# Bias row as the router's 65th row, chosen sets marked by replacement, and a new set-up order in a gated attention and FP4 MLP kernel

## What is computed

```python
q = layernorm(x) @ W_q.T + b_q
scores = (q @ desc_router.T) / sqrt(256)          # 64 sets
scores = where(set named by one of the token's 4 entries, scores, -inf)
keep the two largest; weights = softmax over them
x = x + tanh(g_xattn) * weights @ ctx
h = layernorm(x)
x = x + tanh(g_ffn) * ((gelu_tanh(h @ Wg.T) * (h @ Wu.T)) @ Wd.T)
```

## Time and profile before

| | us |
|---|---|
| median of 3 runs | 310.67 |
| profiled execution | 311.26 |
| its span | 309.5 |

### The profile page before, as it was taken

One profiled execution on the slowest core, in us unless ns is written; L12 is line 12 of the kernel. 1 busy time (PEld: TensorE's weight loads), 2 busy tenths in 40 slices (PEclk: granted clock), 3 DMA queues, 4 the chain that ended last, 5 costly groups with the idle time before them and its releaser, 6 DMA issues.

```text
span 309.5 us, 4648 instructions
## 1 busy us (share of the span) xinstructions
PE 302.0 (98%) x1537; PEld 251.0 (81%) x1537; DVE 223.6 (72%) x478; ACT 155.9 (50%) x287; POOL 144.8 (47%) x138
## 2 busy tenths in 40 slices
PE   6998999999999999999999999999999999999996
PEld 4777888787788788888888888888888888888885
DVE  3999999899985669687676678777676565544545
ACT  3476665657455453435555453444654533444341
POOL 3447455636742342876353325866442233432421
PEclk9999999999999999999999999999999999999999
DMA  6970440020000021326240111424130001110102
GB/s 184 253 186 0 150 124 0 0 37 1 0 2 0 2 34 17 77 57 123 70 101 3 17 17 26 94 53 85 63 94 0 0 15 26 26 40 0 37 0 68
DMA packets 47288, 16.11 MB, mean 52 GB/s; under 512 B 38944, under 2 KB 44448, under 8 KB 47264
## 3 DMA queue, kind: packets, MB, share of 16 engines
q1 hardware_dynamic: 44576, 12.92, 18.0%
q0 software_dynamic: 864, 2.10, 2.5%
q10 hardware_dynamic: 1824, 0.79, 1.1%
HBM read 11.08 MB, written 3.15 MB: 46 GB/s over the span
## 4 chain that ended last, share of the span: by engine, by line
PE 78%; issue 7%; POOL 6%; DVE 4%; ACT 2%; DMA 2%; SPq 0%; DVEq 0%; POOLq 0%
PE ring_ps L1317 49%; PE acc_ps L1351 17%; PE acc_ps L1364 4%; PE att_ps L1364 3%; POOL act_lo L525 3%; POOL w_nat L507 2%; DMA x_sb<-in_x_dram 2%; PE att_ps L1219 1%; POOL w_nat L518 1%; PE ring_ps L1302 1%; ACT act L695 1%; DVE act L1006 0%; DVE act L1000 0%; DVE x_sb L1157 0%; ACT act L691 0%
## 5 line engine op out<-in xcount | busy, mean ns | idle before, releaser
L525 POOL TENSOR_TENSOR act_lo<-act,act_hi 128x512 fp32r<-128x512 f32 x63 | 82.1, 1302 | 118.8 <-ACT act_hi L702 118.6
L1317 PE MATMUL ring_ps<-xt_hi,w_hi 128*128 128x512 f32 (+1 forms) x264 | 103.8, 394 | 1.0 <-ACT xt_hi L675 0.7
L1317 PE MATMUL ring_ps<-xt_hi,w_lo 128*128 128x512 f32 (+1 forms) x264 | 100.9, 384 | 0.0
L1317 PE MATMUL ring_ps<-xt_lo,w_hi 128*128 128x512 f32 (+1 forms) x264 | 100.2, 384 | 0.0
L691 ACT ACTIVATE act<-ring_ps 128x512 f32<-128x512 f32 x64 | 38.1, 596 | 84.2 <-PE ring_ps L1317 83.8
L1000 DVE SCALAR_TENSOR_TENSOR act<-act,ring_ps 128x512 f32<-128x512 f32 x64 | 43.7, 683 | 39.1 <-ACT act L691 38.9
L1006 DVE SCALAR_TENSOR_TENSOR act<-act,ring_ps 128x512 f32<-128x512 f32 x64 | 43.8, 685 | 27.2 <-ACT act L695 25.9
L1317 PEld LDWEIGHTS ring_ps<-xt_hi,w_hi 128*128 128x128 f32 x264 | 49.7, 188 | 11.1 <-issue 1.2
L1317 PEld LDWEIGHTS ring_ps<-xt_lo,w_hi 128*128 128x128 f32 x264 | 49.0, 188 | 10.3 <-DVE xt_lo L938 0.2
L695 ACT ACTIVATE act<-act 128x512 f32<-128x512 f32 x64 | 40.5, 632 | 32.7 <-DVE act L1000 32.7
L1317 PEld LDWEIGHTS ring_ps<-xt_hi,w_lo 128*128 128x128 f32 x264 | 49.8, 188 | 8.3
(11 more groups left out here) (129 smaller groups left out, 331.9 us busy)
## 6 DMA issues: line engine op xcount, KB each, us to landing
x_t<-in_x_dram SPq DMA_DIRECT2D x48, 32.0 KB, 2.1
w_nat<-w_nat SPq DMA_DIRECT2D x96, 16.0 KB
out_dram<-x_sb SPq DMA_DIRECT2D x6, 256.0 KB, 2.2
x_sb<-in_x_dram SPq DMA_DIRECT2D x1, 1024.0 KB, 8.4
ln_dram<-normed SPq DMA_DIRECT2D x16, 64.0 KB, 2.2
w_nat<-ln_dram SPq DMA_DIRECT2D x16, 64.0 KB, 2.0
packed<-L_ffn_gate_W_packed_dram SPq DMA_DIRECT2D x3, 256.0 KB, 2.9
packed<-n_L_ffn_up_W_packed_dram SPq DMA_DIRECT2D x3, 256.0 KB, 3.3
```

The lines of the kernel that those rows point to most:

```text
L525: pool.tensor_tensor(act_lo[:, s % RING, :], act[:, s % ACT_RING, :], act_hi[:, s % RING, :].bitcast(F32), ALU.subtract).then_inc(inter_lo, 1)
L1317: i = pe.matmul(into[:, tok], wt[:, n, w], xt[:, c % 2, k, tok], start=(k, j) == order[0], stop=(k, j) == order[-1])
```

## The change

The b_q row is loaded as row 64 of the router tile, by the second load of ACT's queue, and the tokens by the third instead of POOL's first. The router's transposes now wait for b_q too and give 65 columns; `spread_bias` multiplies the 65th column by the others, and DVE's two instructions on b_q are gone. SCORE_SCALE is halved and later factors doubled.

For sequences 0 to 3, ACT computes tanh(2 s - s0 - s1) of all 64 scores, a half of the tokens at a time, and adds 1 (`soft`); DVE writes CHOSEN over the two largest with two `match_replace` (`marked`; entries 2 to 7 of the eight are set to a spare value that also stands behind the scores), and one instruction takes `soft` where `marked` is CHOSEN. For sequences 4 to 7 the way through indices stays.

The set-up orders of PE, ACT, DVE and POOL are new, with other numbers of zero products. Score(2) moves from unit 2 of the loop into the set-up, ahead of the last first product. Declarations of semaphores and plain slices `0:SETS` are left out below.

```diff
-MASKED = -3.0e38
+MASKED = -1.0e38
+CHOSEN = 2.0e38
+SPARE = 3.0e38
...
-    SCORE_SCALE = float(D) ** -0.5
+    SCORE_SCALE = 0.5 * float(D) ** -0.5
...
-        router_sb = sb("router_sb", [SETS, D])
+        router_sb = sb("router_sb", [SETS + 1, D])
...
-        set_bias = sb("set_bias", [SETS, 1])
-        router_t = sb("router_t", [P, KT, SETS])
+        router_t = sb("router_t", [P, KT, SETS + 1])
...
-        scores = sb("scores", [P, CB, HALVES, SETS])
+        scores = sb("scores", [P, CB, HALVES, SETS + 6])
...
-        picked = choice[:, 0:CB * HALVES * 2 * SETS].rearrange("p (q h k n) -> p q h k n", q=CB, h=HALVES, k=2)
+        soft = choice[:, 0:CB * HALVES * SETS].rearrange("p (q h n) -> p q h n", q=CB, h=HALVES)
+        marked = choice[:, CB * HALVES * SETS:CB * HALVES * SETS + HALVES * (SETS + 6)].rearrange("p (h n) -> p h n", h=HALVES)
...
+        BIAS_AT = KT * (SETS + 1)
...
-            sp.dma_start(router_sb[:, :], router).then_inc(router_loaded, 16)
+            sp.dma_start(router_sb[0:SETS, :], router).then_inc(router_loaded, 16)
...
-            pool.dma_start(tok_sb[:, :, :], token_sets.rearrange("(p h) k -> p h k", h=HALVES)).then_inc(tokens_loaded, 16)
...
+            pool.memset(scores[:, :, :, SETS:], SPARE).then_inc(spares_made, 1)
...
-            for i in range(2):
-                scale_rows_of(1, i)
+            scale_rows_of(1, 0)
+            scale_rows_of(1, 1)
+            root_1(CB)
...
-            root_1(CB)
-            for i in range(2):
-                scale_rows_of(2, i)
+            scale_rows_of(2, 0)
+            scale_rows_of(2, 1)
...
-            sc.dma_start(bq_sb[:, :], b_q.rearrange("(a d) -> a d", a=1).to_broadcast([SETS, D])).then_inc(small_loaded, 16)
+            sc.dma_start(router_sb[SETS:SETS + 1, :], b_q.rearrange("(a d) -> a d", a=1)).then_inc(small_loaded, 16)
+            sc.dma_start(tok_sb[:, :, :], token_sets.rearrange("(p h) k -> p h k", h=HALVES)).then_inc(tokens_loaded, 16)
...
+                q = b % CB
...
-                for k, factor in enumerate((-0.5, 0.5)):
-                    i = sc.activation(lead_tanh[:, b % CB, :, k], lead[:, b % CB, :], ACT.Tanh, scale=factor)
-                i.then_inc(lead_tanh_ready, 1)
+                if b >= BY_ROWS:
+                    for k, factor in enumerate((-1.0, 1.0)):
+                        i = sc.activation(lead_tanh[:, q, :, k], lead[:, q, :], ACT.Tanh, scale=factor)
+                    i.then_inc(lead_tanh_ready, 1)
+                    return
+                for h in range(HALVES):
+                    i = sc.activation(soft[:, q, h, :], scores[:, q, h, 0:SETS], ACT.Tanh, bias=lead[:, q, h:h + 1], scale=2.0)
+                i.then_inc(soft_made, 1)
+                sc.wait_ge(soft_made, b + 1)
+                sc.activation(soft[:, q, :, :], soft[:, q, :, :], ACT.Identity, bias=1.0).then_inc(lead_tanh_ready, 1)
...
                 sc.wait_ge(wq_summed, e + 1)
                 sc.activation(wq_sb[:, e, :], wq_sb[:, e, :], ACT.Identity, bias=wq_sum[:, e:e + 1],
                               scale=-float(D)).then_inc(wq_centered, 1)
-            x_t_out(0)
             sc.wait_ge(score_w_done, 1)
             sc.activation(score_w[:, :, :], acc_ps[:, 1, 0:KT * SETS].rearrange("p (k n) -> p k n", k=KT),
                           ACT.Copy, scale=-SCORE_SCALE / D).then_inc(score_w_copied, 1)
+            x_t_out(0)
             x_t_out(1)
-            lead_out(0)
             compact(0)
             sc.wait_ge(gates_loaded, 16 * 2)
             sc.activation(gates[:, :], gates_in[:, :], ACT.Tanh).then_inc(gates_ready, 1)
+            lead_out(0)
             sc.wait_ge(gates_ready, 1)
             sc.activation(half_gate[:, :], gates[:, :], ACT.Copy, scale=0.5).then_inc(gates_ready, 1)
             probs_out(0)
-            lead_out(1)
             sc.wait_ge(down_scales_loaded, 16)
             sc.activation(scales_sb[:, :, 4:6, :].rearrange("p r a b -> p a r b"), down_scales_sb[:, :, :, :],
                           ACT.Copy).then_inc(down_scales_placed, 1)
+            lead_out(1)
             compact(1)
             rows_high(0)
+            rows_high(1)
             normalise(0)
             probs_out(1)
             ln2_high(0)
-            rows_high(1)
-            x_out(0)
+            down_tile_high(0)
             compact(2)
-            down_tile_high(0)
             normalise(1)
             ln2_high(1)
+            x_out(0)
             square(0)
             rows_high(2)
-            x_out(1)
             tanh(0)
             square(1)
+            x_out(1)
+            rows_high(3)
             tanh(1)
-            rows_high(3)
             for c in range(CHUNKS):
                 for n in range(UNITS):
                     s = c * UNITS + n
...
-                    i = dve.max(top8[:, q, h, :], scores[:, q, h, :])
+                    i = dve.max(top8[:, q, h, :], scores[:, q, h, 0:SETS])
...
-                dve.tensor_tensor(lead[:, q, :], top8[:, q, :, 1], top8[:, q, :, 0], ALU.subtract).then_inc(lead_ready, 1)
+                if b >= BY_ROWS:
+                    dve.tensor_tensor(lead[:, q, :], top8[:, q, :, 1], top8[:, q, :, 0],
+                                      ALU.subtract).then_inc(lead_ready, 1)
+                    return
+                dve.scalar_tensor_tensor(lead[:, q, :], top8[:, q, :, 0], -1.0, top8[:, q, :, 1],
+                                         ALU.mult, ALU.subtract).then_inc(lead_ready, 1)
+                mark(("spares", b), dve.memset(top8[:, q, :, 2:8], SPARE))
...
-                for h in range(HALVES):
-                    i = dve.max_index(top8_at[:, q, h, :], top8[:, q, h, :], scores[:, q, h, :])
-                mark(("top8_at", b), i)
-                after(("top8_at", b))
...
+                    for h in range(HALVES):
+                        i = dve.max_index(top8_at[:, q, h, :], top8[:, q, h, :], scores[:, q, h, 0:SETS])
+                    mark(("top8_at", b), i)
+                    after(("top8_at", b))
...
-                mark(("picked", b), dve.tensor_tensor(
-                    picked[:, q], iota_i[:, :].unsqueeze(1).unsqueeze(1).to_broadcast([P, HALVES, 2, SETS]),
-                    top8_at[:, q, :, 0:2].unsqueeze(3).to_broadcast([P, HALVES, 2, SETS]), ALU.is_equal))
+                if b == 0:
+                    dve.wait_ge(spares_made, 1)
+                after(("spares", b))
+                for h in range(HALVES):
+                    i = dve.match_replace(marked[:, h, :], top8[:, q, h, :], scores[:, q, h, :], CHOSEN)
+                mark(("marked", b), i)
...
-                after(("picked", b))
-                mark(("weighed", b), dve.scalar_tensor_tensor(
-                    picked[:, q], lead_tanh[:, q].unsqueeze(3).to_broadcast([P, HALVES, 2, SETS]), 1.0, picked[:, q],
-                    ALU.add, ALU.mult))
-                after(("weighed", b))
-                dve.tensor_tensor(probs[:, q, :, :], picked[:, q, :, 0], picked[:, q, :, 1], ALU.add).then_inc(probs_ready, 1)
+                after(("marked", b))
+                dve.scalar_tensor_tensor(probs[:, q, :, :], marked[:, :, 0:SETS], CHOSEN, soft[:, q, :, :],
+                                         ALU.is_equal, ALU.mult).then_inc(probs_ready, 1)
...
-                            acc_ps[:, 0, 0:KT * SETS].rearrange("p (k n) -> p k n", k=KT)).then_inc(router_copied, 1)
-            dve.wait_ge(small_loaded, 16)
-            dve.wait_ge(router_loaded, 16)
-            dve.tensor_tensor(bq_sb[:, :], bq_sb[:, :], router_sb[:, :], ALU.mult).then_inc(bias_weighed, 1)
-            dve.wait_ge(bias_weighed, 1)
-            dve.tensor_reduce(set_bias[:, :], bq_sb[:, :], AXIS.X, ALU.add).then_inc(bias_weighed, 1)
+                            acc_ps[:, 0, 0:KT * (SETS + 1)].rearrange("p (k n) -> p k n", k=KT)).then_inc(router_copied, 1)
...
             dve.tensor_scalar(allowed[:, :, :], allowed[:, :, :], 0.5, MASKED, ALU.is_lt, ALU.mult).then_inc(mask_made, 1)
             dve.wait_ge(mask_made, 4)
             dve.wait_ge(bias_done, 1)
-            cb = acc_ps[:, 0, KT * SETS:(KT + 1) * SETS].unsqueeze(1).to_broadcast([P, HALVES, SETS])
+            cb = acc_ps[:, 0, BIAS_AT:BIAS_AT + SETS].unsqueeze(1).to_broadcast([P, HALVES, SETS])
             mark("score_bias", dve.scalar_tensor_tensor(score_bias[:, :, :], cb, SCORE_SCALE, allowed[:, :, :],
                                                         ALU.mult, ALU.add))
+            after("score_bias")
             input_stats(1)
-            after("score_bias")
+            input_variance(1)
             read_scores(0)
             find_top(0)
+            unpack(0, 0)
             find_lead(0)
+            unpack(0, 1)
             find_where(0)
             weigh(0)
-            input_variance(1)
-            for stage in range(3):
-                unpack(0, stage)
+            unpack(0, 2)
             read_scores(1)
             find_top(1)
             find_lead(1)
             update_stats(0)
```

(92 more changed lines are left out.)

6 lines of the change are left out of this document (3 added, 3 removed).

## The result

The changed kernel takes 312.17 us (median of 7 runs, 311.84 to 315.03), the kernel before 310.80 in the runs beside it. The ratio is 1.0068, with a 95% interval of 1.0036 to 1.0099. Forecast was 309.5, range 308.4 to 311.5. The profiled run of after took 312.1 (span 310.3, granted clock 1.00).

The account below looks back on a forecast made before the run. Prediction: PE's own products bound the kernel from 29.7 to 300 us, so only the set-up could gain. gate(2) 1.35 us ahead, less 0.15 for small losses, gave 1.2 and 309.5 us against the median; range 308.4 to 311.5.

Parts of the forecast that it names:

- What is gained there stays gained, one for one, if PE stays busy behind it: Time won in the set-up, ahead of gate(2), was to carry through the PE-busy stretch to the end undiminished.
- part 5: Behind gate(2): POOL's scaling and low part keep 0.5 us of cover each; 0.15 us off for small losses, gain 1.2.
- The base of the sum: The gain was worked out against the profiled run of 311.26 us and taken off the median of 310.67.
- Part 1: Loads and router: b_q row lands at 4.2 us, x some 0.2 earlier; the moved token load costs ACT about 0.5.
- walk: The prediction's step-by-step reckoning of start times through the set-up, ending with gate(2) at 29.35 us.
- Part 2: Sequence 0 up to its weights: a new wait for compact(0) until 10.8 us; weights at 12.65 against 12.90, gain 0.25.
- Parts 3 and 4: Weights to first gate product at 20.45 us, gain 0.48; then to gate(2) at 29.35, gain 1.35.
- Rival A: Set-up: POOL's lock holds both last unpack steps ahead of xt_lo(1); gain only 0.35 us, time 310.3; chance 0.20.
- Rival B: Set-up loads: last down tile lands at 12.5 us instead of 9.9, delaying all behind compact(0); time 312.1, chance 0.13.
- Rival C: Router and x transposes: PE stays at the slower step after twelve zero products, 1.1 us lost; time 310.6, chance 0.07.
- the prediction's 1.0 for score(2): Moving score(2) from the loop to the set-up, ahead of gate(2), was counted as 1.0 us of gain.

Follow-up runs that it names:

- the two traces of before with stand-ins: The kernel before with one or two extra statistics instructions on DVE, on unneeded data, where sequence 6's rows are added: 310.85 and 312.08 us.
- p_tok: The kernel after with eight one-column memsets first on DVE and the token load back at the head of POOL's queue: 311.20 us, ratio 1.0013.
- q_tok15: The kernel after with eight memsets on DVE, fifteen zero products at the start instead of twelve, and tokens first on POOL's queue: 309.70 us, ratio 0.9977.

## Why the prediction was wrong, step by step

- **The step that failed: "What is gained there stays gained, one for one, if PE stays busy behind it", with the 0.15 us that part 5 takes off for small losses.** PE did not stay busy, and the term of 0.15 was 1.4: by the forecast the stretch from gate(2) to the end takes 278.95 us (310.06 less 1.76 and 29.35), and it took 280.33. The prediction looked for new holes in the first chunk, where the change moves work, not at what the number of DVE instructions does 170 us later. Of the 2.67 us between 309.5 and 312.17 this is 1.4, the start of gate(2) at 29.97 instead of 29.35 is 0.6, and the 0.59 between profiled run and median is most of the rest.
- **The base of the sum.** The profiled execution of before was a late one. In it b_q was waited for until 5.98 and x until 6.99; in the two traces of before with stand-ins, whose set-up is the same, until 5.31 and 5.50, and 6.13 both times, and gate(2) starts at 28.85 and 29.04, not at 29.71. Taking a gain against 29.71 off the median counted time that the median has already: 0.7 to 0.9 by these starts, 0.46 by the difference of the two times (311.26 and 310.80).
- **Part 1.** The row of b_q was no wait any more, and the router's transposes ran at 3.93, as forecast. Of the tokens I costed the 0.5 us that their issue takes on ACT, not their own landing: issued at 1.88 in place of 1.27, they were there at 6.89, and the statistics of sequence 0 began at 7.50 (walk: 6.8). This is the mis-sized term of the set-up: from 6.89 DVE works without a wait until it reads the scores at 10.64. Sequence 1's x came at 8.25, not 7.6.
- **Part 2.** The wait for compact(0), which I took for the bound, was not one: compact(0) began at 10.13 (walk 9.95), but the scores were read at 10.64 only, and the codes were there. The ACT step was right (0.59 + 0.31, 1.0 with the handover), and so were the replacements (0.30 each with their load). Weights at 13.02 against 12.65. (Two sums of the walk are 0.1 too high: from 6.8 they come to 9.5 and not 9.6, and 10.8 with 0.25 and 0.16 is 11.2 and not 11.3.)
- **Parts 3 and 4.** The distances held: weights to statistics 2.19 (2.15 and 0.05 said), statistics to shift 1.98 (1.97), first gate product to second half 3.76 (3.95), second half to gate(2) 5.03 (4.95). xt_lo(0) was done at 20.65 instead of 20.0, with 0.52 us of it for the late x of sequence 2, which I had not looked up.
- **Rival A** (both last unpack steps held) did not happen. One was held, as the forecast took it (1.15 us at 23.78; the one before took 0.25), and it cost nothing, since xt_hi(1) was ready only at 24.89.
- **Rival B** (slower through a load) named the wrong load and the wrong price. **Rival C** is real in part of the executions: it costs the runs it hits up to 3 us. Alone it is not seen in the median (310.93 with fifteen products, 310.81 with twelve); with early tokens it is, in p_tok against q_tok15 (311.20 and 309.70), as far as the later start of PE in p_tok is not the cause. After's own trace has the fold at 1.06, so there it cost nothing.
- **The sum.** With tokens and clock mended, gate(2) starts at 28.88: a gain of 0.97 to 1.16 against the two stand-in traces (with the prediction's 1.0 for score(2), which is 0.87 by after's timeline), near the 1.2 of the forecast, and q_tok15's 309.70 is 0.2 from the 309.5. That nearness is in part luck: the base was off, and the wait for compact(0) that the walk names as its bound is a wait in neither trace. The distances of the set-up held. What after lacked for it were the tokens' early place and, in part of its executions, the products at full rate; the gap took the rest.

Not tried: another place for POOL's low part or its output add, which would let the loop bear the gap. That the gap is a fetch of code is not shown. Its place moves with the number of instructions (two gaps, three numbers of memsets), which is shown; the packet behind it only fits, and no run takes a fetch away.

## What to carry to other kernels

Before a gain is taken off a median, ask whether the profiled execution is a typical one in the very stretch that the change shortens. When a load changes queues, cost its own landing and who waits for it. And when a change adds or removes instructions on an engine, compare start-to-start distances of dependent instructions late in the program with those of before: a gap without a wait points at the program's places, and a few idle instructions at the start can move it.

## What the runs showed of the chip

- At certain places of VectorE's program, presumably borders in its code, two dependent instructions stand 0.35 us further apart (a listed idle of 0.46), and eight or sixteen instructions more ahead of them move the place. The Trainium skill's "mostly hidden" (Runtime: NRT & Kernel Launch, Instruction fetch mechanics) agrees with the second gap, at 300.62, which cost nothing; the first cost 1.1 to 1.3 us through the collision behind it.
- Which of two engines passes first can hang on less than 0.1 us: POOL 1.21 us behind the start of the four adds leaves them at 1.67, 1.17 behind makes them 2.74. Sequence 6's loss costs over 1 us of the total, sequence 7's alone 0.2 to 0.4.
- One instruction of 0.41 us between two dependent ones delayed the second by 0.15 us, two by 0.48: the handover between dependent instructions hides part of what is put between them.
- PE can run at little more than half the rate (products of W_q 1.91 us against 1.06, scores 3.68 against 1.96) in rows that show a granted clock of 1.00; the durations tell it, the clock row does not.
